# Two attention blocks over 16 images: operand stacks copied inside SBUF, softmax reciprocals taken in four pieces by VectorE

## The reference

```
block 0: xn = group_norm(x, 32 groups) ; q, k, v = W.xn + b, 4 heads of 32 channels
         w = softmax(q.k / sqrt(128)) over 1024 keys, per head ; h = Wp.(w.v) + bp
         x = (x + h) / sqrt(2)
block 1: h = group_norm(x, 8 groups) ; qkv = W.h + b, one head of 128 channels
         x = x + Wp.(softmax(q.k / sqrt(128)).v) + bp
```

## Time and profile before

| | us |
|---|---|
| median of 3 runs | 1835.58 (1827.13 to 1838.28) |
| profiled execution | 1824.1, its span 1822.1 |

### The profile page before, as it was taken

How to read it: one execution, slowest core, us unless ns; L and a number is a source line. 1 busy time by engine, 2 the same in 40 slices (tenths; PEclk the granted TensorE clock), 3 DMA queues, 4 the chain that set the end, 5 groups by cost and what they waited for, 6 DMA issues and landing times.

```text
span 1822.1 us, 25657 instructions
## 1 busy us (share of the span) xinstructions
PE 1641.6 (90%) x9319; PEld 1082.2 (59%) x9319; DVE 1133.0 (62%) x1897; ACT 1076.8 (59%) x1825; POOL 1096.0 (60%) x503
## 2 busy tenths in 40 slices
PE   3889798989989898998989899998989999889978
PEld 1334365656656665665666566665656666556647
DVE  2666575756767675766767566676756666676232
ACT  1245465656656565665656566565656666556734
POOL 1077676665757666575766657477655747765720
PEclk8598899999999999999999999999999999999989
DMA  6131304140321414032140404114040411300000
GB/s 189 58 70 65 76 19 115 38 122 24 100 58 36 117 36 122 24 111 49 35 127 26 122 25 118 46 42 116 25 122 25 124 39 46 101 24 13 13 12 18
DMA packets 65837, 120.63 MB, mean 66 GB/s; under 512 B 26032, under 2 KB 26672, under 8 KB 65712
## 3 DMA queue, kind: packets, MB, share of 16 engines
q1 hardware_dynamic: 65712, 118.99, 23.3%
HBM read 76.22 MB, written 42.21 MB: 65 GB/s over the span
## 4 chain that ended last, share of the span: by engine, by line
PE 72%; DMA 11%; SPq 5%; DVE 5%; issue 3%; ACT 3%; POOL 0%; ACTq 0%; POOLq 0%; DVEq 0%
PE bank L906 13%; PE acc L846 12%; PE scores L885 11%; PE scores L828 10%; DMA k_stack<-parts_dram 9%; PE scores L872 5%; PE acc L911 3%; PE bank L911 3%; PE scores L864 3%; PE scores L865 3%; PE scores L866 3%; DVE halfmax L711 3%; SPq L432 2%; PE bank L933 2%; PE bank L915 2%
## 5 line engine op out<-in xcount | busy, mean ns | idle before, releaser
L517 POOL TENSOR_TENSOR sum<-sum,probs 128x1024 f32<-128x1024 f32 x448 | 1048.7, 2373 | 467.8 <-PE acc L846 425.0
L711 DVE TENSOR_REDUCE halfmax<-bank 128x1 f32<-128x512 f32 x1024 | 679.6, 686 | 363.7 <-PE bank L906 358.1
L553 ACT ACTIVATE probs<-scores 128x512 f32<-128x512 f32 x896 | 519.3, 600 | 458.2 <-PE scores L828 453.5
L906 PE MATMUL bank<-k_stack,q_stack 96*128 96x512 f32 x1024 | 457.3, 465 | 133.1 <-DMA k_stack<-parts_dram 104.7
L828 PE MATMUL scores<-q_stack,k_stack 97*128 97x512 f32 x1024 | 443.9, 446 | 2.3 <-DMA q_stack<-neg 2.3
L906 PEld LDWEIGHTS bank<-k_stack,q_stack 96*128 96x128 f32 x1024 | 198.4, 198 | 302.6 <-issue 179.8
L885 PEld LDWEIGHTS scores<-v,turned 128*128 128x128 f32 x1952 | 253.8, 192 | 36.9 <-ACT turned L573 17.1
L885 PE MATMUL scores<-v,turned 128*128 128x128 f32 x1952 | 260.7, 277 | 4.6 <-ACT turned L573 3.5
L846 PE MATMUL acc<-probs,v 128*32 128x512 f32 x1792 | 236.6, 642 | 0.0
L828 PEld LDWEIGHTS scores<-q_stack,k_stack 97*128 97x128 f32 x1024 | 197.0, 194 | 62.7 <-issue 37.8
L753 DVE TENSOR_REDUCE negmax<-scores 128x1 f32<-128x1024 f32 x128 | 156.5, 1222 | 59.8 <-PE scores L866 59.5
(11 more groups left out here) (86 smaller groups left out, 1318.9 us busy)
## 6 DMA issues: line engine op xcount, KB each, us to landing
q_stack<-parts_dram SPq DMA_DIRECT2D x96, 256.0 KB, 4.4
k_stack<-parts_dram SPq DMA_DIRECT2D x48, 512.0 KB, 9.4
xin<-x_dram SPq DMA_DIRECT2D x16, 512.0 KB, 3.5
x<-x_dram SPq DMA_DIRECT2D x16, 512.0 KB, 3.6
parts_dram<-q_hi SPq DMA_DIRECT2D x16, 512.0 KB, 2.6
parts_dram<-q_lo SPq DMA_DIRECT2D x16, 512.0 KB, 3.6
parts_dram<-k_hi SPq DMA_DIRECT2D x16, 512.0 KB, 2.6
parts_dram<-k_lo SPq DMA_DIRECT2D x16, 512.0 KB, 3.7
```

The source lines that it names most:

```text
L517: pool.tensor_tensor(total, total, probs[:, ring_slot(i, half, kt), 2 * two:2 * two + 2, :], ALU.add).then_inc(added[two], 1)
L553: act.activation(dst, score_bank(i, index), ACT.Exp).then_inc(exp_done, 1)
L711: dve.tensor_reduce(halfmax[:, h, t, half:half + 1], banks[p][:, :], AX.X, ALU.max).then_inc(bank_free[p][VE], 1)
L906: mm = pe.matmul(dst[:, :], qs[0:SPLIT, q_half(i, arg // FIRST), h, tile(t % 4)], ks[0:SPLIT, i % 2, h, halves(half)], start=True, stop=True)
```

## The change

The parts no longer go to DRAM. `stack_queries` and `stack_keys` copy from the parts in SBUF straight into the stacks, a transfer for each head and group: 12 of 64 KB for a half of the queries (two halves), 12 of 128 KB for the keys, 36 an image. Both DRAM tensors and `put_parts`, `turn_sums` and `spread_reciprocals` are gone, with 9 small transfers for each half of an image. In place of these VectorE takes the reciprocal of `rb` itself, 128 x 512 repeated values in four pieces of 128 x 128 for each half. The table is written anew around these pieces, the maxima are taken in another order of tiles, and rinv stands a gap later. Its core:

```diff
-            ("rinv", t, 0, None, None, first + 3),
+            ("rinv", t, 0, None, None, first + 4),
...
-    ("save", 0, 0, None, 35, None), ("sums", 0, 0, 45, 45, None), ("recip", 0, 0, None, None, 51),
-    ("scale", 0, 0, None, None, 59), ("proj", 0, 0, 61, None, 61), ("stats1", 0, 0, None, None, 61),
+    ("save", 0, 0, None, 35, None), ("sums", 0, 0, 45, 45, None), ("recip", (0, 0), 0, None, None, 46),
+    ("recip", (0, 1), 0, None, None, 50), ("recip", (0, 2), 0, None, None, 52), ("recip", (0, 3), 0, None, None, 53),
+    ("scale", 0, 0, None, None, 59), ("proj", 0, 0, 61, None, 61), ("stats1", 0, 0, None, None, 63),
...
+    ("recip", (1, 0), 0, None, None, GAPS + 9), ("recip", (1, 1), 0, None, None, GAPS + 13),
+    ("recip", (1, 2), 0, None, None, GAPS + 15), ("recip", (1, 3), 0, None, None, GAPS + 15),
...
-        STACK_DMAS = 3
+        STACK_DMAS = 3 * HEADS
...
-            def put_parts(i):
-
-                for n, which in enumerate(("q0", "k0")):
-
-                    for piece in [(which, h, i) for h in range(2)]:
-                        sp.wait_ge(bank_free[bank_of(piece)][VE], given_back(piece))
-                    for k in (2 * n, 2 * n + 1):
-                        sp.dma_start(parts_dram[k], part[k][:, :].bitcast(F32)).then_inc(parts_out, 16)
-
             def stack_queries(i, half):
-                sp.wait_ge(parts_out, 64 * (i + 1))
+
+                for piece in [("q0", h, i) for h in range(2)]:
+                    sp.wait_ge(bank_free[bank_of(piece)][VE], given_back(piece))
                 if 2 * i + half >= 3:
 
                     sp.wait_ge(score_full, 4 * KT * (2 * i + half - 2) + (half == 0))
-                for group, k in enumerate((0, 1, 0)):
-                    sp.dma_start(qs[DH * group:DH * (group + 1), q_half(i, half), :, :].bitcast(F32),
-                                 parts_dram[k][:, halves(half)].rearrange("(h r) n -> r h n", h=HEADS)).then_inc(
-                                     stacked_q[half], 16)
+                hi, lo = part[0:2]
+                for h in range(HEADS):
+                    for group, src in enumerate((hi, lo, hi)):
+                        sp.dma_start(qs[DH * group:DH * (group + 1), q_half(i, half), h, :].bitcast(F32),
+                                     src[head(h), halves(half)].bitcast(F32)).then_inc(stacked_q[half], 16)
 
             def stack_keys(i):
-                for group, k in enumerate((2, 2, 3)):
-                    sp.dma_start(ks[DH * group:DH * (group + 1), i % 2, :, :].bitcast(F32),
-                                 parts_dram[k].rearrange("(h r) n -> r h n", h=HEADS)).then_inc(stacked_k, 16)
+                for piece in [("k0", h, i) for h in range(2)]:
+                    sp.wait_ge(bank_free[bank_of(piece)][VE], given_back(piece))
+                hi, lo = part[2:4]
+                for h in range(HEADS):
+                    for group, src in enumerate((hi, hi, lo)):
+                        sp.dma_start(ks[DH * group:DH * (group + 1), i % 2, h, :].bitcast(F32),
+                                     src[head(h), :].bitcast(F32)).then_inc(stacked_k, 16)
...
-            def recip(half, i):
-                dve.wait_ge(sums_in, 16 * HEADS * (2 * i + half + 1))
-                dve.reciprocal(compact[:, half, :], compact[:, half, :]).then_inc(recip_done, 1)
+            def recip(half, quarter, i):
+                if quarter == 0:
+                    piece = ("sums", half, i)
+                    dve.wait_ge(bank_free[bank_of(piece)][SC], given_back(piece))
+                cut = rb[:, HALF * half + C * quarter:HALF * half + C * (quarter + 1)]
+                dve.reciprocal(cut, cut).then_inc(recip_done, 1)
```

More of the change, by code:

```diff
@@ L87 @@
 NEXT0 = [
-    ("stats0", 0, 2, None, None, 43), ("mean0", 0, 2, 45, None, 45), ("var0", 0, 2, 51, None, 51),
-    ("affine0", 0, 2, None, None, 62), ("norm0", 0, 2, None, GAPS + 1, None),
+    ("stats0", 0, 2, None, None, 40), ("mean0", 0, 2, 46, None, 46), ("var0", 0, 2, 50, None, 50),
+    ("affine0", 0, 2, None, None, 62), ("norm0", 0, 2, None, GAPS + 0, None),
     ("q0", 0, 2, GAPS + 5, GAPS + 5, GAPS + 6), ("q0", 1, 2, GAPS + 6, GAPS + 6, GAPS + 6),
-    ("k0", 0, 2, GAPS + 6, GAPS + 6, GAPS + 6), ("k0", 1, 2, GAPS + 7, GAPS + 7, GAPS + 7),
@@ new lines @@
+    ("scale", 1, 0, None, None, GAPS + 19), ("proj", 1, 0, GAPS + 21, None, GAPS + 21),
+    ("stats1", 1, 0, None, None, GAPS + 21), ("mean1", 0, 0, GAPS + 24, None, GAPS + 24),
+    ("var1", 0, 0, GAPS + 25, None, GAPS + 25), ("affine1", 0, 0, None, None, GAPS + 31),
+    ("norm1", 0, 0, None, GAPS + 33, None), ("q1", 0, 0, GAPS + 36, GAPS + 36, GAPS + 38),
+    ("q1", 1, 0, GAPS + 37, GAPS + 37, GAPS + 38), ("k1", 0, 0, GAPS + 38, GAPS + 38, GAPS + 38),
+    ("k1", 1, 0, GAPS + 38, GAPS + 38, GAPS + 39), ("v1", 0, 0, GAPS + 39, GAPS + 39, None),
@@ L105 @@
+    ("v1", 1, 0, GAPS + 42, GAPS + 42, None),
 ]
@@ L149 @@
     ("out", 1, -1, LAST_AT[KT - 1, -1] + 11, None, LAST_AT[KT - 1, -1] + 11),
[L150 to L153, removed]
+    ("save", 1, -1, None, 4, None), ("sums", 1, -1, 6, 6, None), ("recip", (1, 0), -1, None, None, 7),
+    ("recip", (1, 1), -1, None, None, 7), ("recip", (1, 2), -1, None, None, 7), ("recip", (1, 3), -1, None, None, 7),
+    ("scale", 1, -1, None, None, 7), ("proj", 1, -1, 9, None, 9), ("stats1", 1, -1, None, None, 9),
+    ("mean1", 0, -1, 11, None, 11), ("var1", 0, -1, 12, None, 12), ("affine1", 0, -1, None, None, 14),
+    ("norm1", 0, -1, None, 14, None),
     ("q1", 0, -1, 20, 20, 20), ("q1", 1, -1, 20, 20, 20), ("k1", 0, -1, 21, 21, 21), ("k1", 1, -1, 21, 21, 21),
@@ L426, in load_shift @@
                     "p h (t n) -> p (h t) n", n=C).bitcast(F32), neg[:, :].bitcast(F32)).then_inc(shift_loaded, 16)
-            def turn_sums(i, half):
-                piece = ("sums", half, i)
-                sp.wait_ge(bank_free[bank_of(piece)][SC], given_back(piece))
-                for h in range(HEADS):
-                    sp.dma_start(compact[:, half, KT * h:KT * (h + 1)], rb[DH * h:DH * h + 1, halves(half)].rearrange(
-                        "o (p e) -> o p e", e=KT)).then_inc(sums_in, 16)
-            def spread_reciprocals(i, half):
-                n = 2 * i + half + 1
-                sp.wait_ge(recip_done, n)
-                sp.dma_start(recip_dram[:, halves(half)].rearrange("h (p e) -> p h e", e=KT),
-                             compact[:, half, :].rearrange("p (h e) -> p h e", h=HEADS)).then_inc(recip_out, 16)
-                sp.wait_ge(recip_out, 16 * n)
-                for h in range(HEADS):
-                    sp.dma_start(rb[head(h), halves(half)],
-                                 recip_dram[h:h + 1, halves(half)].to_broadcast([DH, HALF])).then_inc(rb_loaded, 16)
             def store(i, half):
@@ L708, in maximum @@
                 p = bank_of(piece)
-                t, half, h = n // 8, n // 4 % 2, n % 4
+                t, half, h = max_of(n)
                 dve.wait_ge(bank_full[p], filled(piece))
@@ L901, in work @@
                 if name == "max":
-                    t, half, h = arg // 8, arg // 4 % 2, arg % 4
+                    t, half, h = max_of(arg)
                     if arg % FIRST == 0:
```

45 lines of the change are left out of this document (12 added, 33 removed).

## The result

| | before | changed |
|---|---|---|
| median us | 1836.93 (4 runs, 1827.13 to 1839.38) | 2010.47 (4 runs, 2004.39 to 2013.52) |
| ratio, 95% interval | 1 | 1.095 (1.0909 to 1.0991) |
| span us, profiled execution | 1822.1 | 2008.0 |
| granted TensorE clock, mean | 0.945 | 0.909 |
| TensorE busy, idle, us | 1641.6, 180.5 | 1699.6, 308.4 |

I had predicted 1733, and on the slower side a shortage of SBUF ports at 1934 and transfers one after another at 2256. Of the 186 us that the span grew by, 128 are idle time of TensorE and 58 are busy time, the work being the same and its clock lower.

What follows compares the result with a forecast made beforehand. TensorE bounds the kernel, busy 90%, its idle time mostly waits for k_stack. 15 x (-5.97 stall - 2.3 clock + 2.0 reciprocals) = -94, head -4, end -4: -102 us, giving 1733 us as median; range 1697 to 1838.

Steps and rivals of the forecast that it cites:

- a shortage of SBUF ports: Rival at the stack transfers: reading and writing SBUF share a limit, rate halves to 91 GB/s; 1934 us, chance 0.13.
- transfers one after another: Rival at the stack transfers: each of 24 pays its 2.0 us landing singly; 2256 us, chance 0.02.
- Other paths: Passage on GpSimd's (POOL's) chain and the way from the sums to scale: costs nothing, gains nothing inside the rounds.
- some 2 us of air: GpSimd's chain from var0 starts one gap earlier, gaining some 2 us, less 0.9 for a reciprocal; costed at nothing.
- My sum: 15 x (-5.97 - 2.3 + 2.0) = -94 us, head -4, end -4: -102 us, predicting 1733 us.
- The stall for the keys: TensorE's wait for the last transfer into k_stack, 5.97 us an image behind the head, claimed to go wholly.
- the second rival: SP's stack issues bound at 0.83 us each, stacks land at 720.5, the stall stays; 1851 us, chance 0.12.
- Reciprocals: On VectorE: eight pieces of 0.91 us, +6.6 us an image, of which 2 us surfaces.
- The clock: TensorE's clock, lowered behind each stall, returns to 1.00 in the rounds: -2.3 us an image.
- The text on what would show it: Signs of right or wrong; wrong included halfmax waits over 60 us, issues over 0.6 us, or rate under 150 GB/s.

Runs made afterwards that it cites:

- e1: Kernel before, with GpSimd forming x1 one add earlier (after add 20 instead of 21): 2027.96 us, ratio 1.1004.
- e2: Changed kernel, with GpSimd forming x1 one add later (after add 22 instead of 21): 1843.7 us, ratio 1.0026 to before.
- e9: Changed kernel, with VectorE's first multiplication of an image two gaps earlier (57 instead of 59): 1838.0 us, ratio 1.0022 to before.
- e5: Changed kernel, with x1 formed in two halves, behind adds 5 and 22: 1756.21 us, ratio 0.9542 to before.
- e4: Changed kernel, with both multiplications of mix by rb moved from VectorE to GpSimd: 1719.0 us, ratio 0.9338 to before.
- e6: e4, with each half of the queries waiting only for its own parts: 1687.22 us, ratio 0.9169 to before.
- e10: e4, with the stacks by way of DRAM as before and the reciprocals in rb kept: 1808.14 us, ratio 0.9854 to before.
- e8: e4, with each reciprocal taken twice, the first into a spare tile that nothing reads: 1742.01 us, ratio 0.9477 to before.
- e3: Kernel before, with the stacks alone copied inside SBUF, old table and old reciprocals kept: 1877.96 us, ratio 1.021.

## Why the prediction was wrong, step by step

**The step that failed** stands under "Other paths": "`scale` stays at gaps 59 and 19, so inside the rounds this gains nothing", and before it the sentence on GpSimd, whose chain starts a gap earlier and "gets some 2 us of air", costed at nothing. I asked of a kept gap number whether it gains, and never whether it costs. A gap of the table fixes where an instruction stands among VectorE's and TensorE's, not where it stands against GpSimd's. X1's forming moved from 0.74 us behind the first multiplication's issue to 0.61 us ahead of it. That 1.35 us turned 1.31 us into 12.59. e1 and e2, which move the forming alone, and e9, which moves the multiplication alone, show it.

Measured from the score matmul of gap 59 (782.70 in before, 737.75 in the changed kernel), both instructions moved. The forming came at 2.25 us and now comes at 1.53, 0.72 earlier; it stands in the chain that begins with var0, and this is the air of which the prediction spoke. The multiplication was issued at 1.51 and now is at 2.14, 0.63 later, though its gap is the same: the new order of the maxima puts one, at 739.29, between `neg` and it, where in before nothing stood. So the kept gap did not even mean a kept time. Either shift alone would have left the multiplication ahead, by 0.11 or 0.02 us; no run tries them apart.

The second multiplication had been covered by the very stall that the change removes. This is read from the timelines; what it costs is shown by e5 against e2.

The excess over the forecast, in the medians as measured: 2010 with both; 1844 with the first freed (e2); 1756 with both at 2.2 to 3.1 us (e5); 1719 with no lock at all (e4). My sum gave 1733.

**What before's rows held.** The multiplication's least time was 681 ns and its most 10502, in the same program. One at 2.70 us stands in the earlier trace rows, and I read it only for the transfer ahead of it. A most of fifteen times the least, for one shape of instruction, says that something holds it while it counts as busy; I looked for waits between instructions only.

**The stall for the keys: right in the main, and one term too small.** 34.8 us of it are left for 104.7, 11.3 of these in the head, the rest 1.7 us each in the mean (23.5 / 14). The term that was mis-sized is the issue: 0.43 us each by the earlier trace rows, measured 0.59, and 0.63 from one start to the next.

```profile
781.18 1.17 SPq L419 DMA_DIRECT2D k_stack<-k_hi  x2
782.40 0.59 SPq L419 DMA_DIRECT2D k_stack<-k_lo  x1
...
788.31 0.59 SPq L419 DMA_DIRECT2D k_stack<-k_lo  x1
...
791.03 0.47 PE L882 MATMUL bank<-k_stack,q_stack 96*128 96x512 f32 x1 [2.07 <-DMA k_stack<-k_lo]
```

Twenty-four issues from 772.83 to 788.90 take 16.1 us instead of the 10.4 that 0.43 would give, and with the landing TensorE goes on 18.2 us after the first issue; the forecast was 15.6. By its terms: the queries' issues took 8.4 us for 5.2, the keys 7.7 for 8.6 and the last landing 2.1 for 1.8. The keys' data kept pace with their issues, the first landing 1.7 us behind the end of its issue and the last 2.0. So the issues bound, the second rival's mechanism at 70% of its price. e6 buys it back by starting earlier.

**Transfers: rivals refuted.** The last issue ends at 788.90 and the reader runs 2.1 us later, so that the fixed part of the transfers overlaps, and in 24 transfers is paid once. Between 781 and 789 the DMA engines moved 184 GB/s, no less than the 182 of the earlier trace rows. Neither the ports nor a setup cost paid singly shows. The Trainium skill's rule against small pieces (SBUF — State Buffer, section "The DMA setup-cost knee") points the other way from e10 against e4: 13 large transfers an image through DRAM (4 parts, 9 stacks) were 89 us slower than 36 small ones. In e10 a turn-round of 4.4 us stands ahead of the large transfers, so this says nothing against size by itself; no run separates the two.

**Reciprocals: right.** 0.942 us each in the median against 0.91 predicted, and of as many again between a fifth and somewhat over a third surfaces (e8). The divide steps of the Trainium skill (VectorE: DVE Perf Modes, section "First, the fixed hardware budget") gave an estimate of 1.07; the rows were nearer.

**The clock: right.** 1.00 in the windows of e4, where stalls of 1.7 us are left, and of e6, where hardly any is. In two other windows of 100 us of e4's rounds it is 0.93 and 0.98. e4's profiled execution is 103.9 us under that of before in span, where I summed 102. e4 also moves the multiplications from VectorE to GpSimd, and it still has stalls that the sum left out, so this is agreement of the whole and no proof of its terms: part of it is luck.

**The text on what would show it** named waits for `halfmax` over 60 us as the sign of error, and 223 came; but I had tied the sign to reciprocals that fill VectorE. VectorE was indeed full (22.92 of 25 us), but with one instruction that for most of its time did nothing.

## What to carry to other kernels

Before moving work, look at the spread of each instruction's duration on VectorE and GpSimd, not at its mean: a least of 0.68 and a most of 10.5 us for one shape is a wait that no view of waits lists. When a change moves either of two engines that share operands from SBUF, write down which of the two is issued first and by how much, and treat a lead under a microsecond as one that any edit of either list can turn round: here 1.35 us did. If the two-operand work can go to the engine that holds the lock (1.29 us there), its place no longer matters; and a stall that is removed may have been what kept another wait short.

## What the runs showed of the hardware

I took each end of a GpSimd instruction at which a multiplication of VectorE was already waiting, in seven traces (before, changed, e1, e2, e3, e5, e9), and counted whether it got in there:

| what GpSimd does next | got in |
|---|---|
| it pauses | 124 of 124 |
| from an add to x1's forming (one operand), no pause | 76 of 79 |
| from an add to an add, no pause | 17 of 293 |
| from x1's forming to an add, no pause | 0 of 18 |

So VectorE is shut out not for one instruction but for a whole run, 12.6 us in the changed kernel and 13.96 in e1, while GpSimd's adds keep their length (2.3 to 2.4 us). Where it gets in, GpSimd's next instruction is held up in its turn: in all 17 the next add takes 2.80 to 2.82 us. Of the 17, 13 are e9's, always between adds 20 and 21, with the multiplication issued 0.5 us ahead of that end. The lead isn't what lets it in, since in the changed kernel a multiplication issued 0.50 us ahead of such an end (1804.25) stays out. Nor is it a late operand of the next add: its exponentials were ready at least 5.9 us ahead in 16 of the 17, and 2.9 us or more ahead where the multiplication stayed out. What does let it in stays open.

An issue from SBUF to SBUF took 0.59 us of SP in the median in the changed kernel, of a part to DRAM 0.32 to 0.54 by its kind (e10), and from DRAM into a stack 0.43 (e10).
